# Causal attention score tiles: 64 queries of both heads of a pair instead of 128 queries of one head

## The chip, the cores and the metric

The kernel runs on one core of a Trainium2 chip. The metric is the time on the device in microseconds, lower is better. Below, TensorE is the matrix engine (PE in the profile; its weight loads are PEld), VectorE is DVE, ScalarE is ACT, GpSimd is POOL, and SyncE (SP) issues the DMAs.

## What is computed

One macaron block over x of 2 batches x 1024 tokens x 1024 columns, all in fp32: half a feed-forward layer (with a LoRA adapter), latent attention, half a feed-forward layer. The change touches only the attention, which has 32 heads; the essentials are:

```python
q = rmsnorm(x @ wq_a.T) @ wq_b.T              # 64 plain + 64 rotated columns a head
kv = rmsnorm(ckv) @ wkv_b.T                   # keys and values from 64 latents
scores = einsum('bqhd,bkhd->bhqk', q_full, k_full) * softmax_scale
scores = where(causal, scores, min)           # query i sees keys 0..i
out = einsum('bhqk,bkhd->bqhd', softmax(scores), v)
```

## The kernel before

**Stages.** The first feed-forward layer, the latents (shared keys `keyT`, normalised query latents `qnT`), the attention, the output product, and the second feed-forward layer run one after the other. The attention takes from about 358 to 1330 us of the profiled execution. Products that need more than the reduced precision of an `fp32r` operand are done in three passes over a high and a low part (`PASSES`: high x high, low x high, high x low), so each product of `fp32r` operands is three matmuls.

**Steps.** The attention is 32 steps: 16 pairs of heads x 2 batches. A step has these jobs, named by one letter and a number in the tables `PE_STEP`, `ACT_STEP`, `DVE_STEP` and `POOL_STEP` (L895 to L902), which fix by hand the order of work in each engine's queue. Each engine works strictly through its table; "+0", "-1" and "+1" say which step a job belongs to.

- Q0 to Q3 (TensorE, L618, six matmuls of 512 columns each): the queries of one head and one half of the tokens: Q0 is head 0, tokens 0 to 511, Q1 head 1 of the same, Q2 and Q3 the two heads of tokens 512 to 1023. ScalarE copies each out of PSUM with three instructions (L626 to L628). GpSimd rotates it with three (A0 to A3; L633, L635, L637). ScalarE writes the high part into `q` (H0 to H3, L644) and GpSimd the low part (B0 to B3, L648).
- S0 to S15 (TensorE, L1290): score tiles. Tile n is 128 queries of head n % 2, row block t = n // 2, and (t + 1) x 128 keys, at least 256. Tiles of over 512 keys are computed in two pieces, so a step has 24 pieces and 72 matmuls. S0 waits for B0, S1 for B1, S8 for B2 and S9 for B3 (semaphore `q_lo`).
- M0 to M15 (VectorE, L1408): add the causal mask, find the row maximum, copy to SBUF. E0 to E15 (ScalarE, L1357): the exponential and its row sum. T0 to T15 (VectorE, L1418): transposes in 32 x 32 blocks into `pT`.
- V0 to V7 (TensorE, L1307): probabilities times latent values, in 32 x 64 parts of the array with plain fp32 operands; V of row block kt covers the queries from that block on. It takes 256 matmul instructions a step. V0 waits until T15 is done.
- O0 to O3: ScalarE moves the upper half of one PSUM bank (L1372), VectorE adds the two halves (L1443), in two instructions of 256 columns, one for each head. P0, P1 (GpSimd, L1481): scale by the inverse row sums, which come by way of DRAM (SP queue).
- F0, F1, in every second step: folds of the next pair's query weights (TensorE L600, ScalarE L606 and L607, VectorE L611 and L612). W0 (L1316): fold of the output weights, a plain fp32 product.

TensorE's queue in a step reads: S8, F0, S9, F1, Q0, S10, S11, Q1, S12, S13, W0, S14, S15 (the S and F of the step before), then Q2, Q3, S0 to S7, V0 to V7. A bank of PSUM that a job fills must have been emptied: F0 needs O0, F1 needs O1, and Q0 needs the split of F0 in the same bank. VectorE's queue reads O0, M8, O1, F0, M9, O2, T8, and so on. GpSimd's queue is B2, B3, then for the next step A0, A1, B0, B1, then P0, P1, then A2, A3. ScalarE's is F0, F1, E8, Q0, E9, E10, Q1, and so on.

`place(n)` gives a tile's PSUM columns, `emptied(n)` the maxima that must be done before it is written. `q` holds, for each head and part, 1024 queries in a row.

Of the kernel before, what the change touches and what calls it, by code (L numbers as in the profile page):

```python
# [650 lines left out]
def latents_phase(nc, k, src_d, args, ahead, v_d):
# [6 lines left out]
    with ExitStack() as stack:  # L658
# [68 lines left out]
        def _(pool):  # L727
            for g in range(4):
# [5 lines left out]
            diagonal = k.mask[:, S - P:S]  # L734
            nc.gpsimd.affine_select(out=diagonal, in_=diagonal, compare_op=ALU.is_ge, fill=MASKED, base=0,
                                    pattern=[[-1, P]], channel_multiplier=1).then_inc(mask_made, 1)
            pool.wait_ge(mask_made, 1)
# [369 lines left out]
def attention_phase(nc, k, args, oT_d, rinv_d, wvo_d, v_d, src_d, dst_d):  # L1107
# [6 lines left out]
    with ExitStack() as stack:  # L1114
# [27 lines left out]
        def spare(e, t0, t1):  # L1142

            return pT[:, e, t0:t1, CHUNK:S]

        qf, swapped = spare(0, 0, 2), spare(0, 2, 4)
        o_raw, o_scale = spare(1, 0, 2), spare(1, 2, 4)
# [468 lines left out]
```

## Time and profile before

| | us |
|---|---|
| median of three runs | 1893.22 |
| lowest and highest | 1892.95, 1896.05 |
| span of the profiled execution (its only time) | 1895.1 |
| TensorE busy in it | 1803.7 (95%) |
| VectorE, ScalarE, GpSimd busy | 1231.4, 1000.5, 877.8 |
| mean granted clock of TensorE | 0.985 of 2.4 GHz |

A busy share is an average over the stages. In a timeline, matmuls of one line that follow each other are merged to one row; its length runs to the modelled end of the last of them, so the time that a group really takes is read from its start to the start of the next group.

### The profile page before, as it was taken

What the parts mean: (1) busy time and instruction counts of PE and PEld (TensorE: products, weight loads), DVE (VectorE), ACT (ScalarE), POOL (GpSimd) and SP (SyncE); (2) the same over time, 40 slices, a digit from 0 to 9 for tenths busy, and PEclk for the clock granted to TensorE, in tenths of its full rate; (3) what the DMA queues carried; (4) which work ended last, traced back from release to release, by engine and by line L of the source; (5) the groups of instructions that cost most, each with busy time, mean ns of one, the idle gap of its engine ahead of it and who ended that gap; (6) DMA issues with size and microseconds to landing.
All of it is one profiled execution on the core that took longest, in us unless ns stands there. A gap on an engine that the chain in (4) does not pass through costs nothing. (4 is left out here: it accounts for less than half of the span.)

```text
span 1895.1 us, 44298 instructions
## 1 busy us (share of the span) xinstructions
PE 1803.7 (95%) x15472; PEld 1422.9 (75%) x15472; DVE 1231.4 (65%) x2654; ACT 1000.5 (53%) x2137; POOL 877.8 (46%) x641
## 2 busy tenths in 40 slices
PE   5999969899999999999999999998999999989999
PEld 4788869877777777777777777775788888877887
DVE  5655358688898888889888888989521111125453
ACT  2221047788887888888787888877310100112110
POOL 3232112377777878777787878775000000014321
PEclk9999979999999999999999999999999999989999
DMA  6542162311212112121222212123742233224321
GB/s 217 193 156 100 67 173 94 84 62 44 86 59 78 57 62 80 57 80 40 85 69 68 69 51 82 55 86 113 249 151 89 94 100 115 67 87 158 130 89 59
DMA packets 111969, 182.74 MB, mean 96 GB/s; under 512 B 27680, under 2 KB 64672, under 8 KB 109856
## 3 DMA queue, kind: packets, MB, share of 16 engines
q1 hardware_dynamic: 111904, 181.88, 29.8%
q8 instruction: 41, 0.67, 0.2%
q14 instruction: 24, 0.20, 0.0%
HBM read 122.33 MB, written 59.51 MB: 96 GB/s over the span
## 5 line engine op out<-in xcount | busy, mean ns | idle before, releaser
L1290 PE MATMUL psS<-keyT,q 128*128 128x512 f32 (+2 forms) x2304 | 473.2, 350 | 23.9 <-POOL q L648 14.5
L1290 PEld LDWEIGHTS psS<-keyT,q 128*128 128x128 f32 x2304 | 381.2, 189 | 118.2 <-DVE negmax L1408 41.7
L1357 ACT ACTIVATE prob<-prob,negmax 128x640 f32<-128x640 f32 (+7 forms) x512 | 392.0, 767 | 78.5 <-DVE negmax L1408 75.9
L1418 DVE STREAM_TRANSPOSE pT<-prob 128x640 f32<-128x640 f32 (+7 forms) x512 | 379.9, 762 | 66.4 <-PE psV L1307 61.6
L1408 DVE CUSTOM_DVE_ANT_0 prob<-psS,mask 128x640 f32<-128x640 f32 (+7 forms) x512 | 371.9, 742 | 20.9 <-PE psS L1290 7.4
L469 PE MATMUL f_psy<-f_weff,f_xT 128*128 128x512 f32 x1344 | 315.6, 393 | 0.0
L1101 PE MATMUL psS<-o_w,o_o 128*128 128x512 f32 x1344 | 304.8, 389 | 0.0
L469 PEld LDWEIGHTS f_psy<-f_weff,f_xT 128*128 128x128 f32 x1344 | 250.9, 188 | 55.8
L1101 PEld LDWEIGHTS psS<-o_w,o_o 128*128 128x128 f32 x1344 | 252.3, 188 | 52.4
L1307 PE MATMUL psV<-pT,val 32*64 32x512 f32 (+3 forms) x8192 | 264.8, 407 | 6.4 <-DVE pT L1418 6.2
L1307 PEld LDWEIGHTS psV<-pT,val 32*64 32x64 f32 x8192 | 168.8, 132 | 109.7 <-issue 66.2
L633 POOL TENSOR_TENSOR pT<-pT,cosT 64x512 f32<-64x512 f32 x124 | 159.6, 1287 | 194.4 <-ACT pT L628 180.5
L275 POOL TENSOR_TENSOR f_weff<-f_w_in,f_weff 128x1024 fp32r<-128x1024 f32 x16 | 39.0, 2437 | 397.5 <-ACT f_weff L388 397.5
L618 PE MATMUL psV<-qnT,wq 128*128 128x512 f32 x744 | 186.4, 393 | 0.4 <-issue 0.4
L1074 DVE TENSOR_TENSOR o_y<-psS,o_x_in 128x512 f32<-128x512 f32 x32 | 22.0, 691 | 252.0 <-PE psS L1101 238.4
L351 POOL TENSOR_TENSOR f_xo<-f_xt,f_bias_half 128x1024 f32<-128x1024 f32 x32 | 81.4, 2543 | 216.7 <-DMA x<-f_xo 103.5
L1023 ACT ACTIVATE o_o<-o_in 128x1024 fp32r<-128x1024 f32 x32 | 32.6, 1055 | 257.2 <-PE psS L1101 235.8
L648 POOL TENSOR_TENSOR q<-pT,q 128x512 fp32r<-128x512 f32 x124 | 160.1, 1291 | 10.9 <-POOL pT L637 2.2
L635 POOL TENSOR_TENSOR pT<-pT,sinT 64x512 f32<-64x512 f32 x124 | 160.0, 1290 | 9.7
L637 POOL TENSOR_TENSOR pT<-pT 64x512 f32<-64x512 f32 x124 | 159.5, 1286 | 9.7
L618 PEld LDWEIGHTS psV<-qnT,wq 128*128 128x128 f32 x744 | 135.3, 188 | 27.0 <-issue 0.6
L179 ACT ACTIVATE f_xT<-f_ps_xT 128x512 fp32r<-128x512 f32 x64 | 35.0, 595 | 172.6 <-PE f_ps_xT L170 172.6
(120 smaller groups left out, 1919.1 us busy)
## 6 DMA issues: line engine op xcount, KB each, us to landing
wo<-in_wo SPq DMA_DIRECT2D x16, 1024.0 KB, 6.0
pT<-row_scales SPq DMA_DIRECT2D x128, 128.0 KB, 2.9
oT<-pT SPq DMA_DIRECT2D x64, 256.0 KB, 2.5
o_in<-oT SPq DMA_DIRECT2D x32, 512.0 KB, 5.2
f_xt<-in_x SPq DMA_DIRECT2D x16, 512.0 KB, 4.4
f_w_in<-in_w SPq DMA_DIRECT2D x16, 512.0 KB, 6.7
w_sum<-f_w_in SPq DMA_DIRECT2D x16, 512.0 KB, 5.3
x<-f_xo SPq DMA_DIRECT2D x16, 512.0 KB, 3.0
```

The source lines that it names most:

```text
L469: ins = nc.tensor.matmul(psy[:, j, half, :], f.xT[:, j, a, dt, :], weff[:, b, m, dt, half * BANK:(half + 1) * BANK], start=(i == 0 and dt ...
L618: ins = nc.tensor.matmul(bank, self.wq[:, a, e, t, :], qnT[:, m, t, x:x + CHUNK], start=(i == 0 and t == 0), stop=(i == 2 and t == QRT - 1))
L633: nc.gpsimd.tensor_tensor(plain, plain, cos, ALU.mult).then_inc(self.rope_parts, 1)
L635: nc.gpsimd.tensor_tensor(crossed, crossed, sin, ALU.mult).then_inc(self.rope_parts, 1)
L637: nc.gpsimd.tensor_tensor(plain, plain, crossed, ALU.add).then_inc(self.roped, 1)
L648: nc.gpsimd.tensor_tensor(self.rows(LO, n), qf, self.rows(HI, n).bitcast(F32), ALU.subtract).then_inc(self.q_lo, 1)
L1101: ins = nc.tensor.matmul(self.ps[:, j, x], self.o[j][:, a, pair, :], self.w[pair][:, m, x], start=(pair == 0 and i == 0), stop=(pair == PA ...
L1290: ins = nc.tensor.matmul(psS[:, slot, start + x0:start + x1], q[:, e, a, t * P:(t + 1) * P], k.keyT[:, m, b * S + x0:b * S + x1], start=(i ...
L1307: ins = nc.tensor.matmul(out[:, :, kt:QT, :], val[rows, b, block, kt, :], pT[rows, :, kt:QT, x:x + 32], start=(kt == 0 and a == 0), stop=( ...
L1357: nc.scalar.activation(row, row, ACT.Exp, bias=negmax[:, n % 8:n % 8 + 1], scale=-1.0, accum_out=rowsum[:, column(n, s):column(n, s) + 1]) ...
L1408: nc.vector.tensor_tensor_reduce(out=prob[:, n % RING, 0:width], in0=place(n), in1=k.mask[:, S - width:S], scale=-1.0, scalar=LARGEST, op0 ...
L1418: nc.vector.transpose(pT[:, n % 2, t, 0:width], prob[:, n % RING, 0:width]).then_inc(turned, 1)
```

## The change

Tile n is now 64 queries of both heads of the pair (128 rows: 64 of head 0, 64 of head 1), with (n + 1) x 64 keys. A step still has 16 tiles, 24 pieces and 72 matmuls, and S0 to S15, M, E and T keep their places in the four tables. Tiles 0 to 7 are one piece, tiles 8 to 15 two equal pieces of (n + 1) x 32 keys. The columns of a step's tiles fall from 9216 (9472 with the padding of the first two) to 8704; tiles 0, 1 and 2 have 64, 128 and 192. `q` is laid out by tile, so a high or low part of 512 queries is written as eight runs of 64. Since a tile holds both heads, S0 waits for B1 and S8 for B3. V's second inner index covers 32 queries less; the causal mask is made with two selections of 64 x 64 in place of one of 128 x 128; the sums of O are one instruction of 512 columns for a bank. The places of scratch buffers and the addresses of the row scales follow the new order.

```diff
+ROWS = P // 2
+TILES = S // ROWS
...
-        self.q = c.sb("q", [P, 2, 2, S], F32R)
+        self.q = c.sb("q", [P, 2, TILES, 2, ROWS], F32R)
...
-        return self.q[:, n % 2, part, n // 2 * CHUNK:(n // 2 + 1) * CHUNK]
+        return self.q[:, part, n // 2 * QT:(n // 2 + 1) * QT, n % 2, :]
+
+    def by_tile(self, qf):
+
+        return qf.rearrange("p (a r) -> p a r", r=ROWS)
...
-        nc.gpsimd.tensor_tensor(self.rows(LO, n), qf, self.rows(HI, n).bitcast(F32), ALU.subtract).then_inc(self.q_lo, 1)
+        nc.gpsimd.tensor_tensor(self.rows(LO, n), self.by_tile(qf), self.rows(HI, n).bitcast(F32), ALU.subtract).then_inc(self.q_lo, 1)
...
-        pT = c.sb("pT", [P, 2, QT, S])
+        pT = c.sb("pT", [P, TILES, S])
...
+        def columns(n):
+
+            return (n + 1) * ROWS
 
         def place(n):
 
-            t, size = n // 2, (n // 2 + 1) * P
-            if t < 4:
-                return psS[:, n % 4 // 2, n % 2 * BANK:n % 2 * BANK + size]
-            x = P if t == 4 else 0
-            return psS[:, n % 2, x:x + size]
+            if n < QT:
+                x = n % 2 * BANK
+                return psS[:, n % 4 // 2, x:x + columns(n)]
+            x = BANK - columns(n) // 2
+            return psS[:, n % 2, x:x + columns(n)]
...
-                if t % 4 == 0:
-                    pe.wait_ge(q_lo, step * 4 + t // 4 * 2 + e + 1)
-                width = max(2 * P, (t + 1) * P)
-                cut = BANK - P if t == 4 else BANK
-                slot, start = (n % 4 // 2, n % 2 * BANK) if t < 4 else (n % 2, P if t == 4 else 0)
-                pieces = [(0, min(width, cut))] + ([(cut, width)] if width > cut else [])
+                if n % QT == 0:
+                    pe.wait_ge(q_lo, step * 4 + n // QT * 2 + 2)
+                if n < QT:
+                    slot, start, pieces = n % 4 // 2, n % 2 * BANK, [(0, columns(n))]
+                else:
+                    cut = columns(n) // 2
+                    slot, start, pieces = n % 2, BANK - cut, [(0, cut), (cut, 2 * cut)]
                 for x0, x1 in pieces:
-                    x1 = max(x1, x0 + 2 * P)
                     for i, (a, m) in enumerate(PASSES):
-                        ins = nc.tensor.matmul(psS[:, slot, start + x0:start + x1], q[:, e, a, t * P:(t + 1) * P],
+                        ins = nc.tensor.matmul(psS[:, slot, start + x0:start + x1], q[:, a, n, :, :].rearrange("p e r -> p (e r)"),
                                                k.keyT[:, m, b * S + x0:b * S + x1], start=(i == 0), stop=(i == 2))
...
-                            rows, block = slice(32 * i, 32 * i + 32), BLOCKS // 2 * half + a
+                            rows, block, n = slice(32 * i, 32 * i + 32), 2 * a + half, 2 * kt + a
                             x = kt * P + 32 * block
-                            out = psV[KVR * half:KVR * half + KVR, i, :].rearrange("p (e t r) -> p e t r", e=2, r=32)
-                            ins = nc.tensor.matmul(out[:, :, kt:QT, :], val[rows, b, block, kt, :], pT[rows, :, kt:QT, x:x + 32],
+                            out = psV[KVR * half:KVR * half + KVR, i, :].rearrange("p (n r) -> p n r", r=32)
+                            ins = nc.tensor.matmul(out[:, n:TILES, :], val[rows, b, block, kt, :], pT[rows, n:TILES, x:x + 32],
...
-                nc.vector.transpose(pT[:, n % 2, t, 0:width], prob[:, n % RING, 0:width]).then_inc(turned, 1)
+                nc.vector.transpose(pT[:, n, 0:width], prob[:, n % RING, 0:width]).then_inc(turned, 1)
...
-                for e in range(2):
-                    x = slice(e * 32 * QT, (e + 1) * 32 * QT)
-                    halves = [y.rearrange("p (h t r) -> p h t r", h=2, r=32) for y in (psV[0:KVR, bank, x], upper(bank)[:, x])]
-                    ins = nc.vector.tensor_tensor(by_block(o_raw, bank)[KVR * e:KVR * e + KVR], halves[0], halves[1], ALU.add)
-                ins.then_inc(evicted, 1)
+                e = bank // 2
+                halves = [y.rearrange("p (h t r) -> p h t r", h=2, r=32) for y in (psV[0:KVR, bank, :], upper(bank))]
+                nc.vector.tensor_tensor(by_block(o_raw, bank)[KVR * e:KVR * e + KVR], halves[0], halves[1], ALU.add).then_inc(evicted, 1)
```

## Rows read from the trace of the kernel before

**Rows 1.** The page, busy time, share of the span and instructions of the engines.
```profile
PE 1803.7 (95%) x15472; PEld 1422.9 (75%) x15472; DVE 1231.4 (65%) x2654; ACT 1000.5 (53%) x2137; POOL 877.8 (46%) x641
```

**Rows 2.** Timeline of GpSimd, 909 to 949 us: start, length, what, idle before it.
```profile
909.21 2.64 POOL L648 TENSOR_TENSOR q<-pT,q 128x512 fp32r<-128x512 f32 x2 [0.16 <-POOL pT L637]
916.51 1.30 POOL L633 TENSOR_TENSOR pT<-pT,cosT 64x512 f32<-64x512 f32 x1 [4.66 <-ACT pT L628]
...
938.88 2.65 POOL L648 TENSOR_TENSOR q<-pT,q 128x512 fp32r<-128x512 f32 x2
947.45 1.29 POOL L633 TENSOR_TENSOR pT<-pT,cosT 64x512 f32<-64x512 f32 x1 [5.93 <-ACT pT L628]
```

**Rows 3.** Groups of like shape, all of the run: GpSimd's product with cosines.
```profile
L633 POOL TENSOR_TENSOR pT<-pT,cosT 64x512 f32<-64x512 f32 x124 | 159.6, 1287 | 194.4 <-ACT pT L628 180.5 <-POOL pT L637 8.9 <-POOL pT L1481 4.4
```

**Rows 4.** Timeline of TensorE, 909 to 949 us, two steps.
```profile
910.64 1.12 PE L1290 MATMUL psS<-keyT,q 128*128 128x384 f32 x6 [0.39 <-POOL q L648]
912.00 1.13 PE L1290 MATMUL psS<-keyT,q 128*128 128x384 f32 x6 [0.24 <-POOL q L648]
912.96 1.55 PE L618 MATMUL psV<-qnT,wq 128*128 128x512 f32 x6
914.35 2.25 PE L1290 MATMUL psS<-keyT,q 128*128 128x512 f32 x12
916.44 1.54 PE L618 MATMUL psV<-qnT,wq 128*128 128x512 f32 x6
...
920.34 1.08 PE L1316 MATMUL psV<-wo,wv 128*64 128x512 f32 x4
921.35 3.06 PE L1290 MATMUL psS<-keyT,q 128*128 128x512 f32 x12
...
931.59 8.21 PE L1307 MATMUL psV<-pT,val 32*64 32x512 f32 x256
940.21 1.14 PE L1290 MATMUL psS<-keyT,q 128*128 128x384 f32 x6 [0.41 <-POOL q L648]
941.52 0.65 PE L600 MATMUL psV<-wn 64*128 64x64 f32 x4 [0.17 <-DVE pT L1443]
942.10 1.14 PE L1290 MATMUL psS<-keyT,q 128*128 128x384 f32 x6
943.22 0.66 PE L600 MATMUL psV<-wn 64*128 64x64 f32 x4
943.84 1.61 PE L618 MATMUL psV<-qnT,wq 128*128 128x512 f32 x6
```

**Rows 5.** Timeline of ScalarE, same stretch: the last copy of query block 0.
```profile
915.85 0.59 ACT L628 ACTIVATE pT<-psV 32x512 f32<-32x512 f32 x1
```

**Rows 6.** Timeline of VectorE, same stretch, in the step with folds.
```profile
940.55 0.85 DVE L1443 TENSOR_TENSOR pT<-psV,cosT 64x256 f32<-64x256 f32 x2 [0.81 <-ACT cosT L1372]
941.58 0.82 DVE L1408 CUSTOM_DVE_ANT_0 prob<-psS,mask 128x640 f32<-128x640 f32 x1 [0.18 <-PE psS L1290]
...
942.33 0.84 DVE L1443 TENSOR_TENSOR pT<-psV,cosT 64x256 f32<-64x256 f32 x2
943.20 0.29 DVE L611 TENSOR_TENSOR wq<-wpe,wq 128x128 fp32r<-128x128 f32 x1
943.41 0.28 DVE L612 TENSOR_TENSOR wq<-psV,wq 128x128 fp32r<-128x128 f32 x1
```

**Rows 7.** Groups of like shape: VectorE, 1024 keys; a sum of 512.
```profile
L1408 DVE CUSTOM_DVE_ANT_0 prob<-psS,mask 128x1024 f32<-128x1024 f32 x64 | 77.0, 1204 | 1.6
...
L1074 DVE TENSOR_TENSOR o_y<-psS,o_x_in 128x512 f32<-128x512 f32 x32 | 22.0, 691 | 252.0 <-PE psS L1101 238.4 <-DMA o_x_in<-x 10.3 <-PE psS L1088 3.3
```

**Rows 8.** Timeline of TensorE, 338 to 392 us: a transpose group; the first steps.
```profile
338.07 1.03 PE L170 MATMUL l_ps_xT<-ident,l_xn 128*128 128x128 f32 x8
...
382.69 3.75 PE L1290 MATMUL psS<-keyT,q 128*128 128x256 f32 x21 [0.45 <-POOL q L648]
```

**Rows 9.** Timeline of TensorE, the end of the attention.
```profile
1322.11 10.06 PE L1307 MATMUL psV<-pT,val 32*64 32x512 f32 x256 [6.22 <-DVE pT L1418]
```

More of the change, by code:

```diff
@@ L639, in rows @@
     def rows(self, part, n):
-        return self.q[:, n % 2, part, n // 2 * CHUNK:(n // 2 + 1) * CHUNK]
+        return self.q[:, part, n // 2 * QT:(n // 2 + 1) * QT, n % 2, :]
+    def by_tile(self, qf):
+        return qf.rearrange("p (a r) -> p a r", r=ROWS)
     def high(self, nc, qf, n):
-        nc.scalar.activation(self.rows(HI, n), qf, ACT.Copy).then_inc(self.q_hi, 1)
+        nc.scalar.activation(self.rows(HI, n), self.by_tile(qf), ACT.Copy).then_inc(self.q_hi, 1)
     def low(self, nc, pool, qf, n, number):
         pool.wait_ge(self.q_hi, number + 1)
-        nc.gpsimd.tensor_tensor(self.rows(LO, n), qf, self.rows(HI, n).bitcast(F32), ALU.subtract).then_inc(self.q_lo, 1)
+        nc.gpsimd.tensor_tensor(self.rows(LO, n), self.by_tile(qf), self.rows(HI, n).bitcast(F32), ALU.subtract).then_inc(self.q_lo, 1)
 def latents_phase(nc, k, src_d, args, ahead, v_d):
@@ L733, in _ @@
             pool.wait_ge(mask_cleared, 1)
[L734 to L737, printed above, removed]
+            for e in range(2):
+                diagonal = k.mask[e * ROWS:(e + 1) * ROWS, S - ROWS:S]
+                nc.gpsimd.affine_select(out=diagonal, in_=diagonal, compare_op=ALU.is_ge, fill=MASKED, base=0,
+                                        pattern=[[-1, ROWS]], channel_multiplier=1).then_inc(mask_made, 1)
+            pool.wait_ge(mask_made, 2)
             pool.wait_ge(k.tab_in, 48)
@@ L887, in _ @@
             steady(dve, step, NT, 3, 1)
-TILES = 2 * QT
 RING = 8
@@ L967, in __init__ @@
         spots = [("keyT", 0), ("keyT", split), ("q", 0), ("q", split)] + [("prob", split * i) for i in range(4)]
-        spots += [("pT", split * i) for i in (0, 1, 2, 3, 6, 7, 4, 5)]
+        spots += [("pT", split * i) for i in (0, 1, 4, 5, 6, 7, 2, 3)]
         self.w_in = [at(f"o_w_in{j}", "qnT", row * j, [P, D]) for j in range(SLOTS)]
@@ L1140, in attention_phase, with spare @@
         block = stack.enter_context(nc.Block())
[L1142 to L1147, printed above, removed]
-        def place(n):
-            t, size = n // 2, (n // 2 + 1) * P
-            if t < 4:
-                return psS[:, n % 4 // 2, n % 2 * BANK:n % 2 * BANK + size]
-            x = P if t == 4 else 0
-            return psS[:, n % 2, x:x + size]
+        def spare(n):
+            return pT[:, n:n + 2, CHUNK:S]
+        qf, swapped, o_raw, o_scale = spare(0), spare(2), spare(4), spare(6)
+        def columns(n):
+            return (n + 1) * ROWS
+        def place(n):
+            if n < QT:
[3 more added lines that the diff above has]
+            return psS[:, n % 2, x:x + columns(n)]
         def emptied(n):
@@ L1163, in column @@
         def column(n, s):
-            return 2 * QT * (s % 2) + n // 8 * QT + n % 2 * 4 + n // 2 % 4
+            return TILES * (s % 2) + n
         def folds(it, n, s):
@@ L1175, in by_block @@
         def by_block(tile, i):
-            return tile.rearrange("p h (t a r) -> p h t a r", a=BLOCKS, r=32)[:, :, :, i, :]
+            return tile.rearrange("p h (t a r) -> p h t a r", a=2, r=32)[:, :, :, i % 2, :]
         @block.sync
@@ L1200, in turn_scales @@
                 step, x = it * 2 + s, 2 * QT * (s % 2) + QT * ch
-                rows = rinv_d[bass.ds(step, 1), ch * S:(ch + 1) * S].rearrange("a (c q) -> (a c) q", q=P)
+                rows = rinv_d[bass.ds(step, 1), ch * S:(ch + 1) * S].rearrange("a (e c q) -> e (a c) q", e=2, q=ROWS)
                 sp.wait_ge(r_turned, step * 2 + ch + 1)
@@ L1205, in turn_scales @@
                         sp.wait_ge(scaled, step * 2 + ch - 1)
-                    sp.dma_start(rows[:, 32 * g:32 * g + 32], rinvT[32 * g + x:32 * g + x + QT, x // QT, :]).then_inc(r_stored, 16)
+                    sp.dma_start(rows[g // 2, :, g % 2 * 32:g % 2 * 32 + 32], rinvT[32 * g + x:32 * g + x + QT, x // QT, :]).then_inc(r_stored, 16)
                 sp.wait_ge(r_stored, step * 128 + ch * 64 + 64)
@@ L1344, in query_hi @@
             def query_hi(it, n, s):
-                step, row = it * 2 + s, (4 * (n // 2) + 3) * 2 + n % 2
+                step, row = it * 2 + s, QT * (n // 2) + QT - 1
                 act.wait_ge(queries.roped, step * 4 + n + 1)
@@ L1351, in exponentials @@
             def exponentials(it, n, s):
-                step, width = it * 2 + s, (n // 2 + 1) * P
+                step, width = it * 2 + s, columns(n)
                 act.wait_ge(maxed, step * TILES + n + 1)
@@ L1402, in maxima @@
             def maxima(it, n, s):
-                li, width = (it * 2 + s) * TILES + n, (n // 2 + 1) * P
+                li, width = (it * 2 + s) * TILES + n, columns(n)
                 dve.wait_ge(scored, li + 1)
@@ L1412, in transposes @@
             def transposes(it, n, s):
-                step, t, width = it * 2 + s, n // 2, (n // 2 + 1) * P
+                step, width = it * 2 + s, columns(n)
                 dve.wait_ge(exped, step * TILES + n + 1)
                 if later(step, 1):
-                    dve.wait_ge(valued, (step - 1) * QT + t + 1)
-                nc.vector.transpose(pT[:, n % 2, t, 0:width], prob[:, n % RING, 0:width]).then_inc(turned, 1)
+                    dve.wait_ge(valued, (step - 1) * QT + n // 2 + 1)
+                nc.vector.transpose(pT[:, n, 0:width], prob[:, n % RING, 0:width]).then_inc(turned, 1)
             def row_scales(it, ch, s):
```

2 lines of the change are left out of this document (1 added, 1 removed).

## The prediction

> **What bounds the kernel now.** I read the page first: TensorE is busy 95% of the span, every other engine far less [rows 1]. That invites the reading that each matmul column saved is time saved. The timelines say otherwise. GpSimd's comes next [rows 2]. It is the engine with the lowest share, yet from 916.51 to 941.53 us (938.88 + 2.65) it works without a pause worth naming: the ten jobs A0, A1, B0, B1, P0, P1, A2, A3, B2, B3, 25.02 us in all. Then it stands idle for 5.92 us, and before that for 4.66 us, and both times what ends the idle time is ScalarE's last copy of the query block Q0 (L628). Over the run this wait sums to 180.5 us [rows 3], over 31 steps 5.8 us each, a little more than these two because of the first step. TensorE's timeline shows what lies in that pause [rows 4]. B3 ends at 909.21 + 2.64 = 911.85 us; S9, which waits for it, starts at 912.00; Q0, queued behind S9, starts at 912.96; ScalarE's third copy of it ends at 915.85 + 0.59 = 916.44 [rows 5], and A0 starts at 916.51. So there is a ring: B3, S9, Q0, copy, A0 to B3. Its length is 4.66 + 25.02 = 29.68 us in a step without folds, and TensorE needs 29.57 us from S8 to S8 (910.64 to 940.21). In the step with folds it is 5.92 + 25.02 = 30.94 us. The ring is the period; TensorE is nearly as long, but waits 0.39 us at S8 and 0.24 us at S9.
>
> **What a column costs.** From starts in rows 4: Q0 takes 912.96 to 914.35, 1.39 us for six matmuls of 512, 0.232 us each. S10 and S11 (six of 512, six of 256) take 914.35 to 916.44, 2.09 us, so one of 256 takes 0.117 us. That is 0.45 ns a column. A matmul of 288 columns then takes 0.131 us, one of 320 takes 0.146 us.
>
> **The change in the ring.** S8 now holds both heads, so it waits for B3 instead of B2. S8 was done beside B3; now it comes after B3 and before S9 and Q0.
> - Step without folds: old, B3 to Q0 is 912.96 - 911.85 = 1.11 us, of which 0.15 us is the release and 0.96 us is S9 (three of 384, three of 256: 0.88 us by the prices, and 0.08 us for the first after a wait). New: 0.15 + 0.08 + S8 at 6 x 0.131 = 0.79 + S9 at 6 x 0.146 = 0.87, together 1.89 us. That is **+0.78 us**.
> - Step with folds: B3 ends at 941.53, Q0 starts at 943.84, 2.31 us later. Here Q0 waits for VectorE's split of F0, which is queued behind O0, M8 and O1 [rows 6], and M8 needs S8. From S8's start to M8 is 941.58 - 940.21 = 1.37 us, less 192 columns at 0.45 ns: 1.28 us. M8 takes 942.33 - 941.58 = 0.75 us, less 64 columns at (1204 - 820) / 384 = 1.0 ns [rows 6, 7]: 0.69 us. O1 took 0.87 us (942.33 to 943.20) in two instructions of 256; as one of 512, for which the nearest row has 0.69 us [rows 7] against 0.84 us for two, I take 0.72 us. F0's split to Q0 stays 0.64 us. Sum: 0.15 + 1.28 + 0.69 + 0.72 + 0.64 = 3.48 us, **+1.17 us**. If VectorE were not in the way, TensorE's own order (S8, F0 0.58, S9, F1 0.62) would give 0.15 + 0.87 + 0.58 + 0.87 + 0.62 = 3.09 us, +0.78; that is the lower bound.
>
> The ring is run through 30 times (S8 of steps 1 to 30, half with folds): 15 x 0.78 + 15 x 1.17 = 29.3 us.
>
> **What is saved, and why it is worth nothing.** All of this lies beside the ring, on engines that wait for it.
> - TensorE, tiles 3 to 15: the old tiles from the fifth on had 8448 columns, the new from the fifth on 8064; 384 x 3 passes x 0.45 = 0.52 us a step.
> - Tiles 0 to 2: no row shows an `fp32r` product under 256 columns. Below, eight instructions with 128 weight columns and 128 moving columns take 1.03 us, at most 0.13 us each [rows 8], no less than one of 256; I take 0.12 us, no gain. Above, plain fp32: the output fold, 512 columns with its two column halves side by side, takes 920.34 to 921.35, 1.01 us against 0.232 us. At that 4.4-fold rate 128 and 192 columns take 0.25 and 0.38 us, 3 x (0.13 + 0.26) = +1.2 us a step.
> - V: 512 of 9216 columns less, of 8.21 us: 0.46 us.
> - VectorE: 512 columns less in M and in T, and four sums at 0.15 us: 1.6 us. ScalarE: less as well, in E.
>
> TensorE comes to S8 at 910.25 and would now find B3 unfinished for 1.6 us, and with its savings for 2.6 us. Even the +1.2 us of the narrow tiles, and the 0.35 us by which S0 is late because it waits for B1 (S1 waited for it before [rows 8]), stay inside that. The O sums, H2 and H3 come before the new wait or have their inputs as early as now. GpSimd's ten jobs are unchanged in size. The new runs of 64 in `q` have no row: below, a copy made faster by them has no reason; above, eight separate starts at the 0.06 us between two L648 (2.64 - 2 x 1.29) would add 7 x 0.06 x 4 = 1.7 us a step, 50 us. I take nothing, since all is one instruction over the same 512 elements. The address changes of the row scales move as many bytes in as many DMAs.
>
> **The ends.** The last step is VectorE's: TensorE waits 6.22 us for T15 [rows 9]. M8 of that step starts 1.2 us later than before, the chain behind it is 0.9 us shorter, V is 0.5 us shorter: -0.2 us. In the first step, where GpSimd has its queries already, I estimate -0.8 us from the shorter tiles. Both -1 us.
>
> **Sum.** 29.3 - 1 = +28.3 us. The profiled execution has a span of 1895.1 us, 1.9 us (0.1%) over the median of 1893.2 us; on the median the forecast is **1921.5 us**.
>
> **A page against the rows.** The Trainium skill, page "TensorE: Matmul & The Clock Gate", section "Back-to-back issue gap", gives a warm matmul as its columns over 2.4 GHz plus 2.5 ns. By that S8 would take 0.74 us in place of 0.79 us, and the sum would be 1.5 us less; the trace's 0.117 us for 256 columns, against 0.109 by the page, decides for 0.79. The same page, section "LDWEIGHTS (loading the stationary operand)", gives a weight load as its columns over 1.2 GHz, 107 ns for 128. That speaks against the true widths: a tile of 64 columns would be no faster than the load before it. No row here shows such a tile.
>
> **Rivals.**
> 1. *TensorE is the bound, and its columns are time.* For it: 95% busy and waits of only 0.63 us a step. Against it: the ring matches both periods. It decides if B3 is done before TensorE reaches S8, which needs a ring over 2 us shorter than I read. Then each of 31 steps saves 0.52 + 0.46 us, 30 us: 1863 us. If the narrow tiles also cost as plain fp32, each step is 0.2 us longer instead: 1899 us. In a sentence of its own: by the gap rule of the skill's page above, 64, 128 and 192 columns would cost 29, 56 and 83 ns, and this case would come to about 1846 us.
> 2. *The ring grows by its lower bound only*, with VectorE out of the way: 30 x 0.78 - 1 = 22 us, 1916 us.
> 3. *GpSimd's low parts are slower in runs of 64.* Every microsecond in B0 to B3 is in the ring. At a quarter of the upper price, 12 us more: 1934 us; at all of it 1972 us.
>
> **How the numbers follow.** The forecast with rival 2, which differs from it only in size, has 0.74 (of it 0.15 for the lower bound). Rival 1 has 0.13, 0.11 of it faster and 0.02 near 1899. Rival 3 has 0.09. A partial offset that ends near no change has 0.04. A measurement can tell 0.2%, 3.8 us, from no change. Faster by more: 0.11; within: 0.04; slower by more: 0.85. The range reaches down to 1901, past the lower bound of the ring, and up to 1936, over a quarter of rival 3's price; it leaves out rival 1 and the top of rival 3.
>
> **What would show it.** Right: S8 starts 0.15 us after the second L648 of its pair, with an idle time of TensorE of some 2 to 2.6 us a step that GpSimd's L648 ends; GpSimd's pause before L633 grows from 4.66 and 5.92 us to about 5.4 and 7.1 us while its ten jobs still take 25.0 us; V falls by 0.4 to 0.5 us. L648 still takes 1.29 us. The prediction is wrong if S8 starts without a wait for L648, if the pause does not grow, if TensorE's time from S0 to V0 outgrows the ring, or if the ten jobs change their length.

## The result and the profile after

The changed kernel takes 1936.4 us (median of 4 runs, 1931.9 to 1939.4), the kernel before 1893.1 us: a ratio of 1.022, 95% interval 1.020 to 1.024, 43 us slower. The profiled executions have spans of 1934.9 and 1895.1 us. The profiled one of before is 2 us above its median, so the traces show 40 of the 43 us. The forecast was 1921.5 us: the sign is right, the loss is 15 us larger.

The page after, busy time and TensorE's granted clock in 40 slices (tenths of full speed):

```profile
PE 1791.6 (93%) x15472; PEld 1431.6 (74%) x15472; DVE 1186.2 (61%) x2526; ACT 985.2 (51%) x2137; POOL 875.0 (45%) x642
...
PEclk9999989999999999999999999999899999999999
```

TensorE has 12 us less busy time and 40 us more span against [rows 1]; GpSimd's busy time is 875.0 us, 3 us less. The slices are too coarse for the clock; a finer view comes below. TensorE's timeline, a step without folds (start, length, what, idle before it):

```profile
859.85 7.81 PE L1316 MATMUL psV<-pT,val 32*64 32x512 f32 x256
869.34 1.91 PE L1299 MATMUL psS<-keyT,q 128*128 128x288 f32 x12 [1.68 <-POOL q L654]
871.08 1.55 PE L620 MATMUL psV<-qnT,wq 128*128 128x512 f32 x6
...
882.11 2.89 PE L620 MATMUL psV<-qnT,wq 128*128 128x512 f32 x12
885.67 2.06 PE L1299 MATMUL psS<-keyT,q 128*128 128x64 f32 x15 [0.67 <-POOL q L654]
```

GpSimd's timeline, same step:

```profile
866.58 2.62 POOL L654 TENSOR_TENSOR q<-pT,q 128x512 fp32r<-128x512 f32 x2 [0.16 <-POOL pT L639]
874.63 1.30 POOL L635 TENSOR_TENSOR pT<-pT,cosT 64x512 f32<-64x512 f32 x1 [5.44 <-ACT pT L630]
```

B3 ends at 866.58 + 2.62 = 869.20 us, S8 starts at 869.34. V is 7.81 us, 0.40 less than in [rows 4], so TensorE comes to S8 early and stands idle 1.68 us. GpSimd's pause before A0 is 5.44 us where [rows 2] have 4.66. From B3's end to Q0's start it is 1.88 us, forecast 1.89, before 1.11. The same place in a step with folds at full clock (TensorE; VectorE; GpSimd):

```profile
457.13 1.06 PE L1299 MATMUL psS<-keyT,q 128*128 128x288 f32 x6 [1.67 <-POOL q L654]
...
458.71 1.15 PE L1299 MATMUL psS<-keyT,q 128*128 128x320 f32 x6
459.83 0.66 PE L602 MATMUL psV<-wn 64*128 64x64 f32 x4
460.42 1.65 PE L620 MATMUL psV<-qnT,wq 128*128 128x512 f32 x6
...
459.10 0.68 DVE L1451 TENSOR_TENSOR pT<-psV,cosT 64x512 f32<-64x512 f32 x1
...
459.90 0.28 DVE L614 TENSOR_TENSOR wq<-psV,wq 128x128 fp32r<-128x128 f32 x1
...
454.46 2.62 POOL L654 TENSOR_TENSOR q<-pT,q 128x512 fp32r<-128x512 f32 x2
464.07 1.30 POOL L635 TENSOR_TENSOR pT<-pT,cosT 64x512 f32<-64x512 f32 x1 [6.99 <-ACT pT L630]
```

B3 ends at 457.08, Q0 starts at 460.42: 3.34 us, forecast 3.48, before 2.31. But what Q0 follows here is not what the forecast named. F0's split ends at 460.18, 0.24 us ahead of Q0. TensorE's F1 (459.83) starts 0.05 us after O1's end (459.78), and Q0 starts as soon as F1 is through.

The groups of like shape, all of the run (count, busy us, mean ns, idle before and its releasers):

```profile
L1299 PE MATMUL psS<-keyT,q 128*128 128x384 f32 (+11 forms) x2304 | 458.1, 348 | 78.9 <-POOL q L654 63.5 <-DVE negmax L1417 13.5 <-PEq L664 1.6
...
L635 POOL TENSOR_TENSOR pT<-pT,cosT 64x512 f32<-64x512 f32 x124 | 159.9, 1289 | 236.6 <-ACT pT L630 223.0 <-POOL pT L639 8.6 <-POOL pT L1488 4.4
...
L654 POOL TENSOR_TENSOR q<-pT,q 128x512 fp32r<-128x512 f32 x124 | 159.0, 1283 | 12.4 <-POOL pT L639 2.1 <-ACT q L650 1.9
```

GpSimd's wait for the copy of Q0 has grown from 180.5 [rows 3] to 223.0 us. The low parts take 1283 ns each. TensorE's idle time ahead of the score tiles is 78.9 us; the page of before has for it:

```profile
L1290 PE MATMUL psS<-keyT,q 128*128 128x512 f32 (+2 forms) x2304 | 473.2, 350 | 23.9 <-POOL q L648 14.5
```

**Where the 40 us of the spans come from.** I took the starts of the V groups of the first 31 steps from either trace. First to last: 907.86 us before, 950.04 us after, so +42.2 us lies in the 30 steps, and start and end give back 2.4 us. Most steps fall on two values:

| step, us | before | after | difference | forecast |
|---|---|---|---|---|
| without folds | 29.55 | 30.26 | +0.71 | +0.78 |
| with folds | 30.97 | 31.95 | +0.98 | +1.17 |

Fifteen of each give 25 us. The other 17 us are in nine single steps (seven of 34.1 to 34.5, one of 33.5, one of 31.8 us, less 1.7 us that two steps behind them win back), and these have another cause. Busy time by stretch, for the step at 860 us, the next one and the one after it (PE, PEld, DVE, ACT, POOL busy, then the granted clock, DMA share, GB/s):

```profile
860.00:890.10 30.10, 27.41 (x356) 21.05 (x351) 24.44 (x55) 24.01 (x54) 22.83 (x19) 1.00 0.24 79
890.10:924.50 34.40, 32.22 (x365) 24.86 (x364) 25.66 (x61) 24.85 (x59) 23.25 (x19) 0.90 0.15 48
924.50:954.80 30.30, 27.61 (x357) 21.21 (x356) 24.63 (x57) 24.29 (x55) 23.03 (x19) 1.00 0.24 79
```

In the middle step the granted clock is at 1.2 GHz, half of full speed, for 6.8 us (901.1 to 908.0). TensorE's timeline shows where:

```profile
890.11 7.81 PE L1316 MATMUL psV<-pT,val 32*64 32x512 f32 x256
899.56 1.06 PE L1299 MATMUL psS<-keyT,q 128*128 128x288 f32 x6 [1.64 <-POOL q L654]
...
901.13 1.97 PE L1299 MATMUL psS<-keyT,q 128*128 128x320 f32 x6
903.03 1.11 PE L602 MATMUL psV<-wn 64*128 64x64 f32 x4
904.07 2.93 PE L620 MATMUL psV<-qnT,wq 128*128 128x512 f32 x6
906.80 2.73 PE L1299 MATMUL psS<-keyT,q 128*128 128x352 f32 x12
```

The clock falls 1.5 us behind the end of the new idle 1.64 us. S9 then takes 1.97 us where the step at 457.13 has 1.15, and Q0 2.93 us where it has 1.65. S9 and Q0 are in the ring, so the loss is passed on: GpSimd's pause in this step is 9.49 us in place of 6.99:

```profile
908.99 1.30 POOL L635 TENSOR_TENSOR pT<-pT,cosT 64x512 f32<-64x512 f32 x1 [9.49 <-ACT pT L630]
```

Behind its start, where both kernels have one, and ahead of its end, the attention after has seven such stretches of 6.8 us and two of 3.4 us. The kernel before has none between 364 and 1319 us (granted clock 1.00).

### The profile page after: what moved, and what is told of

It is laid out like the page before. It is cut to its first block and busy times, and to the rows that moved or that the text cites. A ratio compares the mean times of both kernels' runs of the same rounds, so it can differ in the third digit from the quotient of the medians.

```text
span 1934.9 us, 44095 instructions
## 1 busy us (share of the span) xinstructions
PE 1791.6 (93%) x15472; PEld 1431.6 (74%) x15472; DVE 1186.2 (61%) x2526; ACT 985.2 (51%) x2137; POOL 875.0 (45%) x642
## 5 line engine op out<-in xcount | busy, mean ns | idle before, releaser
L1299 PE MATMUL psS<-keyT,q 128*128 128x384 f32 (+11 forms) x2304 | 458.1, 348 | 78.9 <-POOL q L654 63.5
L1366 ACT ACTIVATE prob<-prob,negmax 128x64 f32<-128x64 f32 (+15 forms) x512 | 378.2, 740 | 108.8 <-DVE negmax L1417 106.2
L1417 DVE CUSTOM_DVE_ANT_0 prob<-psS,mask 128x64 f32<-128x64 f32 (+15 forms) x512 | 356.4, 711 | 96.8 <-PE psS L1299 89.5
L1427 DVE STREAM_TRANSPOSE pT<-prob 128x64 f32<-128x64 f32 (+15 forms) x512 | 363.0, 729 | 75.8 <-PE psV L1316 63.7
L635 POOL TENSOR_TENSOR pT<-pT,cosT 64x512 f32<-64x512 f32 x124 | 159.9, 1289 | 236.6 <-ACT pT L630 223.0
L1316 PE MATMUL psV<-pT,val 32*64 32x512 f32 (+7 forms) x8192 | 253.4, 397 | 6.8 <-DVE pT L1427 6.0
L1316 PEld LDWEIGHTS psV<-pT,val 32*64 32x64 f32 x8192 | 164.8, 132 | 104.3 <-issue 66.5
L620 PE MATMUL psV<-qnT,wq 128*128 128x512 f32 x744 | 196.5, 408 | 0.4 <-issue 0.4
L654 POOL TENSOR_TENSOR q<-pT,q 128x512 fp32r<-128x512 f32 x124 | 159.0, 1283 | 12.4 <-POOL pT L639 2.1
L620 PEld LDWEIGHTS psV<-qnT,wq 128*128 128x128 f32 x744 | 142.9, 196 | 29.3 <-issue 0.7
L181 ACT ACTIVATE f_xT<-f_ps_xT 128x512 fp32r<-128x512 f32 x64 | 34.9, 595 | 171.6 <-PE f_ps_xT L172 171.6
```

Of the source, the lines that this page charges most:

```text
L620: ins = nc.tensor.matmul(bank, self.wq[:, a, e, t, :], qnT[:, m, t, x:x + CHUNK], start=(i == 0 and t == 0), stop=(i == 2 and t == QRT - 1))
L635: nc.gpsimd.tensor_tensor(plain, plain, cos, ALU.mult).then_inc(self.rope_parts, 1)
L654: nc.gpsimd.tensor_tensor(self.rows(LO, n), self.by_tile(qf), self.rows(HI, n).bitcast(F32), ALU.subtract).then_inc(self.q_lo, 1)
L1316: ins = nc.tensor.matmul(out[:, n:TILES, :], val[rows, b, block, kt, :], pT[rows, n:TILES, x:x + 32], start=(kt == 0 and a == 0), stop=(kt ...
L1366: nc.scalar.activation(row, row, ACT.Exp, bias=negmax[:, n % 8:n % 8 + 1], scale=-1.0, accum_out=rowsum[:, column(n, s):column(n, s) + 1]) ...
L1417: nc.vector.tensor_tensor_reduce(out=prob[:, n % RING, 0:width], in0=place(n), in1=k.mask[:, S - width:S], scale=-1.0, scalar=LARGEST, op0 ...
```

## The experiments

Each run was timed beside the kernel before, which was 1893 to 1895 us in all of them. Steps are given as "without / with folds".

**1. The wait alone.** The kernel before, in which S8 waits for B3 and nothing else is changed:

```diff
-pe.wait_ge(q_lo, step * 4 + t // 4 * 2 + e + 1)
+pe.wait_ge(q_lo, step * 4 + t // 4 * 2 + (2 if t == 4 else e + 1))
```

> The kernel before with its old tiles, and one wait changed: S8 waits for the low parts of both heads (B3) as in the change. Ring theory: S8 leaves its place beside B3 and comes between B3 and Q0. Step without folds: 0.15 + 0.08 + 0.88 + 0.88 = 1.99 us in place of 1.11, +0.88; step with folds: 0.15 + 1.37 + 0.75 + 0.87 + 0.64 = 3.78 in place of 2.31, +1.47 at most. 15 steps of each: +35 us, plus what a lower granted clock takes if TensorE's new idle time brings it (up to some 20 us): 1928 to 1948 us. Theory that the new tiles themselves cost the time (narrow products, or low parts in runs of 64): this kernel has neither, so within 4 us of 1893.

Measured: 1942.7 us, ratio 1.025 (1.021 to 1.028). Steps at full clock 30.48 / 32.24, and 35.0 in ten steps with the clock down. The group line:

```profile
L1290 PE MATMUL psS<-keyT,q 128*128 128x512 f32 (+2 forms) x2304 | 479.9, 356 | 58.0 <-POOL q L648 44.7 <-DVE negmax L1408 7.4 <-PEq L658 1.6
```

One wait, with no column moved, makes all of the loss (49 us, the change has 43), and the clock's part of it too. From B3's end to Q0's start it is 1.98 us and 3.69 us at full clock, expected 1.99 and 3.78. The tiles' shape is not needed for the loss.

**2. The narrow tiles at 256 keys.** The changed kernel with `x1 = max(x1, x0 + 2 * P)` for the piece, so that tiles 0 to 2 compute 256 columns as before (the surplus is not read).

> The kernel after with its first three tiles computed at 256 columns again. Theory that narrow fp32r products are dear: faster than the kernel after, by up to 1.2 us a step where TensorE is waited for. Ring theory: nine matmuls a step change from about 0.113 to 0.118 us and lie beside GpSimd's work, so no change beyond 3 us, 1933 to 1940 us.

Measured: 1940.6 us, 1.025 (1.023 to 1.028), just above the expected 1940; steps 30.3 / 32.0, and ten of 34.2 to 34.6 with the clock down. At full clock the true widths change nothing; the 4 us over the changed kernel go with one more long step. The starts in the trace of the changed kernel say why: inside a tile, matmuls of 64, 128 and 192 columns follow each other every 0.112 to 0.113 us, of 256 every 0.118 to 0.119, of 288 every 0.132, of 320 every 0.146. Under 256 columns the time hardly falls. The Trainium skill, page "TensorE: Matmul & The Clock Gate", section "LDWEIGHTS (loading the stationary operand)", gives a weight load as its columns over 1.2 GHz, 107 ns for 128. The 0.112 us measured here sits just above it; no run shows that the load is the cause.

**3. Work in place of idle time.** The changed kernel with six matmuls of 512 columns ahead of S8's wait; their result is overwritten by S8:

```diff
+                if n == QT:
+                    for i in range(6):
+                        nc.tensor.matmul(psS[:, 0, 0:BANK], k.keyT[:, HI, 0:P], k.keyT[:, HI, 0:BANK], start=True, stop=True)
                 if n % QT == 0:
                     pe.wait_ge(q_lo, step * 4 + n // QT * 2 + 2)
```

> The kernel after, and ahead of S8's wait for B3 six more matmuls of 512 columns whose result is overwritten (1.36 us of work in the 1.65 us in which TensorE stands idle). Clock theory: the stretches of the attention at a granted clock of 0.5 (nine steps of 31.8 to 34.5 us in place of 30.3 and 31.95) disappear, about 19 us less than the kernel after: 1914 to 1921 us, and the rest of the loss, the ring's, stays. If the clock does not depend on that idle time: as the kernel after, 1932 to 1940 us, or a little slower.

Measured: 1918.0 us, 1.013 (1.011 to 1.015). TensorE's timeline and the group line:

```profile
854.41 7.81 PE L1319 MATMUL psV<-pT,val 32*64 32x512 f32 x256
862.15 1.65 PE L1292 MATMUL psS<-keyT 128*128 128x512 f32 x6
863.82 1.93 PE L1302 MATMUL psS<-keyT,q 128*128 128x288 f32 x12
...
L1302 PE MATMUL psS<-keyT,q 128*128 128x384 f32 (+11 forms) x2304 | 447.5, 342 | 35.2 <-POOL q L654 21.1 <-DVE negmax L1420 12.2 <-PEq L664 1.6
```

The steps stay at 30.2 / 32.0, S8 starts no earlier, but only one stretch of 3.4 us at 1.2 GHz is left between the attention's start and its end. Useless work made the kernel 18 us faster. What remains, 24 us, is the ring (forecast 29.3) and the ends.

**4. Q0 ahead of S8.** The changed kernel with the orders of TensorE, ScalarE and VectorE rewritten so that S8 and S9 leave the ring:

```diff
-PE_STEP = ("S8-1 F0-1 S9-1 F1-1 Q0+0 S10-1
+PE_STEP = ("F0-1 Q0+0 S8-1 F1-1 S9-1 S10-1
-ACT_STEP = ("F0-1 F1-1 E8-1 Q0+0 E9-1
+ACT_STEP = ("F0-1 Q0+0 F1-1 E8-1 E9-1
-T7+0 O0-1 M8+0 O1-1 F0+0 M9+0 O2-1
+T7+0 O0-1 F0+0 O1-1 M8+0 M9+0 O2-1
```

> The kernel after with Q0 taken out of the ring: TensorE's order F0, Q0, S8, F1, S9 in place of S8, F0, S9, F1, Q0, with ScalarE's and VectorE's tables to match (F0, Q0, F1, E8; O0, F0, O1, M8). Q0 then no longer stands behind S8's wait for B3, and GpSimd can go on after ScalarE's copy of Q0, which waits for B2 alone. Ring theory: the ring shrinks to about 26 us, TensorE becomes the bound at some 28 us a step without folds and 29.5 with, and the low clock goes: 1845 to 1865 us. Theory that TensorE's own work or the clock makes the change slow: no faster than 1915 us.

Measured: 1971.2 us, 1.040 (1.039 to 1.042). A miss; steps 30.24 / 34.8 to 37.0. TensorE's timeline in a step with folds:

```profile
658.17 0.65 PE L602 MATMUL psV<-wn 64*128 64x64 f32 x4 [1.56 <-DVE pT L1451]
660.00 2.90 PE L620 MATMUL psV<-qnT,wq 128*128 128x512 f32 x6 [1.18 <-DVE wq L614]
```

F0 and Q0 write banks of V that are free only when O0 has read them, 1.5 us after V; with S8 behind them nothing fills that time. S8 ahead of Q0 was cover as well as cost. In steps with folds Q0 waits for F0's split on top, and the clock falls in each of the 15; those without folds never see it fall. The run does not test whether a shorter ring is faster, since the new waits (1.5 us in a step without folds) took the place of the old one.

**5. S0's wait alone.** The kernel before, in which S0 waits for B1 (`2 if t == 0 else e + 1`).

> The kernel before, and S0 alone waits for the low parts of both heads (B1), as in the change; S8 and S9 as before. Ring theory: TensorE gets to S0 up to 0.4 us later, which the wait at S8 takes up: no change beyond 4 us, 1890 to 1898 us. If every lost overlap on TensorE counted, 31 x 0.35 = 11 us: 1904 us.

Measured: 1904.6 us, 1.006 (1.004 to 1.008), a miss. Steps 29.54 / 31.63: nothing without folds, +0.66 us with them. There TensorE's timeline has

```profile
627.65 2.23 PE L1290 MATMUL psS<-keyT,q 128*128 128x256 f32 x15 [0.48 <-POOL q L648]
```

and 0.66 x 15 is the 10 us. In the step with folds that follows, S8 no longer waits for GpSimd and F0 waits for O0:

```profile
642.30 0.65 PE L600 MATMUL psV<-wn 64*128 64x64 f32 x4 [0.33 <-DVE pT L1443]
```

I read this as a chain from S0 through V, O0, the folds and F0's split to Q0 that has no slack before the change in steps with folds, and has some without; no run tests it. In the changed kernel S8 waits 1.67 us for B3 behind that V, so there this chain has slack.

**6 and 7. GpSimd's scaling of the outputs in its pause.** P0 and P1 ahead of A0 (2.6 us a step), and O0 to O3 together ahead of M8 so that P0 can run; on the changed kernel (6) and on the kernel before (7):

```diff
-POOL_STEP = ("B2+0 B3+0 A0+1 A1+1 B0+1 B1+1 P0-1 P1-1 A2+1 A3+1")
+POOL_STEP = ("B2+0 B3+0 P0-1 P1-1 A0+1 A1+1 B0+1 B1+1 A2+1 A3+1")
-T7+0 O0-1 M8+0 O1-1 F0+0 M9+0 O2-1 T8+0 F1+0 M10+0 M11+0 T9+0 O3-1
+T7+0 O0-1 O1-1 O2-1 O3-1 M8+0 F0+0 M9+0 T8+0 F1+0 M10+0 M11+0 T9+0
```

> The kernel after with the scaling jobs P0 and P1 (2.7 us of GpSimd) taken out of the ring into GpSimd's pause: its order is B2, B3, P0, P1, A0, A1, B0, B1, A2, A3, and VectorE does O0 to O3 before M8, in the 1.45 us in which it now stands idle. Ring theory: A0 to B3 takes 22.3 us in place of 25.0, B3 is done when TensorE comes to S8, TensorE's own order becomes the bound at about 28.5 us a step without folds and 30.0 with, and the low clock goes since its idle time at S8 goes: 1855 to 1875 us, faster than both kernels. If what slows the change is not the ring, no gain beyond the 19 us of the clock: 1917 us or more.

> The same two moves on the kernel before. Its ring shrinks too, but S8 stood beside B3 anyway, and its four O jobs take 3.4 us in place of 2.7 and now stand before M8. TensorE's order at 28.9 us a step without folds: 1870 to 1895 us. Against e6 it shows what the new tiles are worth where TensorE is the bound: 0.52 us of score columns and 0.4 us of V a step, some 30 us, so e6 should be the faster by 10 to 35 us.

Measured: 1934.0 us (1.021, 1.020 to 1.023), steps 30.29 / 32.3 (33.5 with the clock down), and 1991.4 us (1.051, 1.050 to 1.053), steps 31.1 or 32.3 / 34.9. Two misses, and run 6 is 57 us the faster of the two where 10 to 35 were expected. By its number run 6 falls to the expectation's other theory, that the ring is not what slows the change. GpSimd's timeline of run 6, step without folds:

```profile
676.44 2.63 POOL L654 TENSOR_TENSOR q<-pT,q 128x512 fp32r<-128x512 f32 x2 [0.37 <-ACT q L650]
681.91 2.66 POOL L1488 TENSOR_TENSOR pT<-pT 128x512 f32<-128x512 f32 x2 [2.85 <-DVE pT L1451]
685.43 1.30 POOL L635 TENSOR_TENSOR pT<-pT,cosT 64x512 f32<-64x512 f32 x1 [0.86 <-ACT pT L630]
...
698.29 1.28 POOL L635 TENSOR_TENSOR pT<-pT,cosT 64x512 f32<-64x512 f32 x1 [1.90 <-ACT pT L630]
```

The pause is filled, and the step is still 30.29 us: A2 now waits 1.90 us for the copy of Q2, which ScalarE makes after E15. That is a second way back from S8 to B3 (S8, Q0 to S15, E15, Q2's copy, A2, A3, B2, B3), nearly as long as the first. TensorE still waits for L654, 0.81 us at S8 and 1.19 us at S0 in this step, so the waits are still GpSimd's. In run 7 the four sums ahead of M8 cost more than they free; TensorE waits for F0's split in steps with folds and, at S10, for M8 in steps without:

```profile
871.71 2.77 PE L618 MATMUL psV<-qnT,wq 128*128 128x512 f32 x6 [2.27 <-DVE wq L612]
...
905.41 3.75 PE L1290 MATMUL psS<-keyT,q 128*128 128x512 f32 x12 [1.81 <-DVE negmax L1408]
```

**8 and 10. Both ways shortened.** As run 6, with F0's split ahead of M8 and with Q2 and its copy ahead of S14 and E14; on the changed kernel (8) and on the kernel before (10). The 5.0 us for P0 and P1 in the expectation is a slip, they take 2.6 us:

```diff
-O0-1 M8+0 O1-1 F0+0 M9+0 O2-1 T8+0 F1+0 M10+0 M11+0 T9+0 O3-1
+O0-1 O1-1 F0+0 O2-1 O3-1 M8+0 M9+0 T8+0 F1+0 M10+0 M11+0 T9+0
-W0-1 S14-1 S15-1 Q2+0 Q3+0
+W0-1 Q2+0 S14-1 S15-1 Q3+0
-H1+0 E14-1 E15-1 Q2+0 Q3+0
+H1+0 Q2+0 E14-1 E15-1 Q3+0
```

> The changed kernel with three moves in the written orders: the output's low parts P0, P1 go ahead of A0 on GpSimd (they then fill its pause), F0's split goes ahead of M8 on VectorE, and Q2 with its copy goes ahead of S14 and E14. Theory (two rings of nearly one length, both through B3, S8 and Q0; the second one comes back through E14, E15, Q2, Q2's copy and A2): the first ring loses the 5.0 us of P0 and P1 less the wait for O3, the second the 1.4 us of E14 and E15 with S14 and S15, and the steps with folds the 1.2 us that Q0 waited for the split of F0. Steps of about 29.0 and 30.5 us in place of 30.3 and 32.3, 1865 to 1890 us if the clock holds. Rival (once the rings are shorter, another chain, through the row maxima that now come after four O sums, sets the same period): steps of 30 us or more, TensorE's idle time put down to VectorE, 1925 us or more.

> The kernel before with the same three moves as the run on the changed kernel. Theory: the same gain, from steps of 29.55 and 30.97 us, but TensorE alone needs 29.2 us a step, so not below about 29.3 and 30.3 us: 1870 to 1895 us, and the changed kernel with the moves is at least as fast since its tiles have fewer columns. Rival (row maxima late behind four O sums): 1925 us or more.

Measured: 1956.8 us (1.032, 1.030 to 1.034), steps 31.39 / 33.04, and 2015.3 us (1.063, 1.061 to 1.065), steps 34.4 / 34.2: the rival's size in both. TensorE in run 8:

```profile
914.30 1.06 PE L1299 MATMUL psS<-keyT,q 128*128 128x288 f32 x6 [0.78 <-POOL q L654]
...
927.44 1.65 PE L620 MATMUL psV<-qnT,wq 128*128 128x512 f32 x6 [0.78 <-ACT wvo L1373]
```

S8 waits 0.78 us in place of 1.64, but Q2 now waits for the copy that frees W0's bank, and the row maxima hold S4 and S5 for another 1.15 us (0.58 + 0.57) in the step without folds ahead of it and 1.49 us (0.91 + 0.58) in this one. The rival put that down to the four sums. Run 6 has the same four sums and waits only 0.4 us a step for row maxima, as the changed kernel does, so on the changed kernel it rather goes with Q2's move, which makes S14, S15 and their maxima late. On the kernel before, the sums have a part in it (run 7).

**9. F0's split first.** The changed kernel with `O0-1 F0+0 M8+0 O1-1` in place of `O0-1 M8+0 O1-1 F0+0`. By the forecast the split stands in the ring behind M8 and O1.

> The changed kernel with one move: on VectorE the split of F0 goes ahead of M8 and O1. Theory (in steps with folds the ring goes through F0's split, which stands behind M8 and O1): F0's split no longer waits for these two, so Q0 starts 0.7 to 1.0 us earlier in 15 of 30 steps, steps without folds stay at 30.3 us, steps with folds go from 31.95 to about 31.1 us: 10 to 15 us less than the changed kernel, 1918 to 1928 us. Rival (F0's product, its copy by ScalarE and S9 hold Q0 anyway, and M8 is now late): steps with folds stay at 32 us or grow, 1934 to 1945 us.

Measured: 1955.9 us, 1.033 (1.030 to 1.036). A miss: steps 30.25 / 33.27, or 35.9 with the clock down. VectorE's and TensorE's timelines:

```profile
979.51 0.29 DVE L613 TENSOR_TENSOR wq<-wpe,wq 128x128 fp32r<-128x128 f32 x1 [2.45 <-ACT wq L609]
...
981.33 0.66 PE L602 MATMUL psV<-wn 64*128 64x64 f32 x4 [1.28 <-DVE pT L1451]
```

At full clock, as here, VectorE stands 2.45 us with M8 and O1 queued behind the split, and TensorE's F1 waits 1.28 us for O1. Q0 starts behind F1, 1.9 us after the split that was moved is done. So the ring of the changed kernel goes through O1 and F1, not through the split, and the move delayed the very job that Q0 follows. Steps without folds, which have no split, do not change.

**11. The scaling given to VectorE.** The changed kernel, P0 and P1 (2.6 us on GpSimd) on VectorE ahead of T0 of the next step, Q2 ahead of S15, its copy ahead of E14:

```diff
-P0-1 P1-1 A2+1 A3+1
+A2+1 A3+1
-M4+0 M5+0 T0+0
+M4+0 M5+0 P0-2 P1-2 T0+0
-S14-1 S15-1 Q2+0 Q3+0
+S14-1 Q2+0 S15-1 Q3+0
-H1+0 E14-1 E15-1 Q2+0 Q3+0
+H1+0 Q2+0 E14-1 E15-1 Q3+0
```

> The changed kernel with the scaling of the outputs (P0 and P1, 2.6 us a step on GpSimd) given to VectorE, where it stands before T0 of the next step in a stretch in which VectorE waits for V, and with Q2 ahead of S15 on TensorE and its copy ahead of E14 on ScalarE. Theory (two rings of nearly one length through B3, S8 and Q0, one by A0 and all GpSimd jobs, one by E15, Q2's copy, A2, A3, B2, B3): the first loses 2.6 us, the second 1.5 to 2.5 us, none of the earlier moves' costs (O sums ahead of the row maxima, a split that waits) is paid, and the period falls to TensorE's own 28.5 to 29.2 us without folds and about 30.5 with them: 1860 to 1885 us, less than the kernel before. Rival (a third chain, through the row maxima, the O sums and the banks of V, has the same length): steps of 30 us or more with TensorE's idle time put down to VectorE or ScalarE, 1915 us or more.

Measured: 1943.2 us, 1.025 (1.023 to 1.027). A miss, steps 30.33 / 31.95. ScalarE's and GpSimd's timelines:

```profile
898.11 0.67 ACT L1366 ACTIVATE prob<-prob,negmax 128x448 f32<-128x448 f32 x1 [2.31 <-DVE negmax L1417]
...
898.78 0.61 ACT L650 ACTIVATE q<-pT 128x512 fp32r<-128x512 f32 x1
...
899.54 2.62 POOL L654 TENSOR_TENSOR q<-pT,q 128x512 fp32r<-128x512 f32 x2 [1.92 <-ACT q L650]
909.15 1.30 POOL L635 TENSOR_TENSOR pT<-pT,cosT 64x512 f32<-64x512 f32 x1 [6.99 <-ACT pT L630]
```

With 2.6 us less to do, GpSimd waits 1.92 us before B2, for H2, which stands behind E6 on ScalarE, and E6 waits 2.31 us for its row maximum. A third way. The text of run 12 below has two slips: it names H3 and B3 for this wait, and it has 1.4 us for P0 and P1 on VectorE, which take 2.5 us (1.26 us each on average). TensorE's idle time goes to L654 and to the row maxima both, so the rival is right only in part.

**12. H2 and H3 ahead of E6 as well,** now on the kernel before, for a version that beats both.

> The kernel before with the outputs' scaling P0 and P1 on VectorE ahead of T0 of the next step, Q2 ahead of S15 and its copy ahead of E14, and the high parts H2 and H3 ahead of E6 on ScalarE (in the last run on the changed kernel B3 waited 1.9 us for H3, which stood behind E6 and E7). Theory (the period of the kernel before is set by rings through GpSimd, TensorE is next with some 28.9 us of its own a step without folds): the waits for L648 go, steps of 29.0 to 29.2 us and 30.3 to 30.5 us in place of 29.55 and 30.97, 1875 to 1885 us. Rival (VectorE, with 1.4 us more a step just ahead of T0, now holds TensorE through the row maxima of S4 and S5): steps without folds of 29.6 us or more, TensorE idle 0.8 us or more for the row maxima, 1895 to 1915 us.

Measured: 1939.0 us, 1.024 (1.023 to 1.026), the rival's wait at a larger price. Steps 30.09 / 32.32. TensorE's timeline:

```profile
885.16 0.79 PE L1290 MATMUL psS<-keyT,q 128*128 128x384 f32 x3 [0.62 <-DVE negmax L1408]
886.55 2.18 PE L1290 MATMUL psS<-keyT,q 128*128 128x384 f32 x9 [0.60 <-DVE negmax L1408]
```

TensorE waits for L648 once in the attention (0.5 us), and GpSimd has 6.8 us of pause and more, so the ring is open. In its place TensorE waits 1.2 us a step for the row maxima. S15 is later by Q2's 1.4 us and VectorE has the scaling, 2.4 us, on top; which of the two does it was not told apart. No run beat the kernel before.

## Why the prediction came out as it did

- **The ring** (forecast +0.78 and +1.17 us a step, 29.3 us): measured +0.71 and +0.98 us, 25 us. Runs 1 and 3 show it: the wait alone makes the loss, and with the clock held it is what is left (24 us at 1918.0). The sum from B3 to Q0 was 1.89 us and measured 1.88. In steps with folds it was 3.48 and measured 3.34: the release took 0.05 us and not 0.15, O1 0.60 and not 0.72, and the last stretch to Q0 0.72 and not 0.64. There the path was wrong at its end: Q0 follows F1, which O1 holds, and not F0's split (run 9). The ten jobs took 24.8 to 25.0 us, up to 0.1 us less than before, which is the rest.
- **That the savings are worth nothing:** right. V fell by 0.40 us, TensorE's busy time by 12 us although some of it ran at half clock, and all of it became wait. Rival 1 needed a B3 that is ready when TensorE comes; it was 1.65 us late.
- **TensorE's idle time for L648** (2 to 2.6 us a step forecast): 1.64 to 1.68 at S8, and 0.67 us at S0 for B1 (thought 0.35), 2.3 us together.
- **S0's lateness "stays inside":** right in the changed kernel. In a step with folds B3 to Q0 (3.34 us), Q0 to A0 (3.65) and the ten jobs (24.96) add up to the whole 31.95 us, and S8 waits 1.67 us for B3. It is not free by itself: alone, in run 5, it costs 0.66 us in each step with folds.
- **Runs of 64** (nothing taken, 50 us as the upper bound): 1283 ns against 1291 before. Rival 3 is out.
- **The narrow tiles** (0.12 us taken, plain fp32 as the upper bound): 0.112 to 0.113 us, hardly less than at 256 columns; rival 1's dear variant is out. So is the 1846 us that the prediction works out from the gap rule: the Trainium skill, page "TensorE: Matmul & The Clock Gate", section "Back-to-back issue gap", says itself that the rule under-counts small matmuls in a stream with weight loads, and the 0.112 us measured here, against 29, 56 and 83 ns by the rule, agree.
- **The ends** (-1 us forecast): -2.4 us.
- **The missing term: the granted clock.** The prediction had TensorE idle for over 1.6 us a step and priced that at nothing beyond the ring. This is the step that failed: that idle time beside the ring costs nothing. Nine stretches at 1.2 GHz followed, 17 us. Run 3 filled the idle time at S8, left the steps at full clock as they were, and got back 18 us, so this is shown.
- **That the time lies no further off** is luck. The ring was put 4 us too high and the ends 1.4 us, which hides part of the 17 us. The median of 1936.4 us lies at the range's upper end of 1936, within the spread of its own runs, and the range reached so far up only for rival 3, which did not come.

What the runs do not settle: why the clock falls in some steps and not in others with the same idle time (eight of the nine long steps are ones with folds), and whether some other order reaches below 1893 us. That a shorter ring makes the kernel faster was not shown either: no reordered kernel was faster than the kernel before, and only run 6 came out (by 2 us, within the spread) below the changed one. The forecast's ring was called *the* period. By the traces of runs 6, 11 and 12 there are other ways round, through Q2's copy, through H2 and through the row maxima, and steps without folds come out at 30.29 us in run 6 and 30.33 in run 11, against 30.26 in the changed kernel, and at 30.09 in run 12 against 29.55 in the kernel before. These ways are read from traces; each was met when another was shortened, none was tested alone.

## What to carry to other kernels

- Follow a semaphore that will be waited for later, or for more, back to the engine that gives it, and see whether that engine's own next input depends on the waiter. If so, the whole delay is added to the period, however idle the engine looks (GpSimd is at 46% here) and however much work the change saves elsewhere.
- A wait put into a step-by-step loop can cost twice when it makes TensorE idle: once as time, once as granted clock in the work behind it. It need not: run 12 has 1.2 us a step in two waits and stays at 2.4 GHz from 361 to 1350 us. Look at the clock by stretches of a step, not at the mean (0.985 against 0.974 here).
- In an order written out by hand, one move frees one chain only; before moving a job, list what is queued behind it on each engine. Where two inputs of a job come nearly together (before the change Q0 starts 0.15 us after the split's end, and F1 takes all of the 0.62 us ahead of it), see which of them the change moves: after it, Q0 follows F1 alone.
